# Attention block of a fused attention and convolution kernel: q.k products summed by adding DMAs, residual rows added by DMA, eight tiles in flight

## What is computed

```python
xn = groupnorm(x); xc = einsum('bchw,oc->bohw', xn, ciw) + cib
t  = xc as tokens (8 batch, 4096 pixels, 64 channels) + pe
tn = layernorm(t); q, k, v = tn @ wq.T + bq, ...; q2, k2, v2 = q @ wiq.T + biq, ...   # 8 heads of 8
scores = einsum('inhd,jnhd->nhij', q2, k2) / sqrt(8)      # for each pixel n: 8 images i against 8 images j
z  = softmax(scores) @ v2 ; z = z @ wout.T + bout ; t = z + t
a  = layernorm(t) @ w1.T + b1 ; g = t @ w2.T + b2
t  = a * gelu(g) @ w3.T + b3 + t
x  = einsum('bchw,oc->bohw', t, cow) + cob + x            # the residual
for _ in range(3):
    x = x + (conv(relu(conv(x, w1) + b1), w2) + b2) / 3
return relu(x)
```

## Time and profile before

| | us |
|---|---|
| median of 3 runs | 1139.01 |
| lowest, highest | 1138.61, 1140.38 |
| span of the profiled execution | 1136.3 |
| set-up block | 0 to 44.3 |
| attention block | 44.3 to 604.7 |
| convolutions | 604.7 to 1136.3 |

### The profile page before, as it was taken

How to read it: one execution, slowest core, us unless ns; L and a number is a source line. 1 busy time by engine, 2 the same in 40 slices (tenths; PEclk the granted TensorE clock), 3 DMA queues, 4 the chain that set the end, 5 groups by cost and what they waited for, 6 DMA issues and landing times. The chain is left out here.

```text
span 1136.3 us, 21019 instructions
## 1 busy us (share of the span) xinstructions
PE 1071.2 (94%) x7238; PEld 601.7 (53%) x7238; DVE 1039.7 (92%) x1475; ACT 652.5 (57%) x1525; POOL 510.7 (45%) x422
## 2 busy tenths in 40 slices
PE   4269999999999999999999999999999999999996
PEld 3156787778777777777653333333333333333331
DVE  5459999999999999999988999999999999999996
ACT  4568889888888888888743233253244242342333
POOL 5134564456445544554452424435345344444440
PEclk9999999999999999999999999999999999999998
DMA  8110111111111111110000000030001100030003
GB/s 303 54 37 21 39 29 35 32 39 29 33 35 38 29 31 38 38 29 20 20 20 1 1 1 1 1 75 1 1 1 34 41 1 1 1 74 1 1 1 74
DMA packets 87545, 35.83 MB, mean 32 GB/s; under 512 B 70210, under 2 KB 86851, under 8 KB 86931
## 3 DMA queue, kind: packets, MB, share of 16 engines
q1 hardware_dynamic: 85634, 33.81, 11.1%
q0 software_dynamic: 768, 0.33, 0.2%
q10 hardware_dynamic: 1040, 0.35, 0.1%
HBM read 26.09 MB, written 8.39 MB: 30 GB/s over the span
## 5 line engine op out<-in xcount | busy, mean ns | idle before, releaser
L1173 ACT ACTIVATE y<-banks,cols 128x1024 f32<-128x1024 f32 x96 | 110.3, 1208 | 259.8 <-PE banks L1165 259.8
L900 POOL TENSOR_TENSOR rstd<-var,half 128x8 f32<-128x8 f32 x32 | 80.8, 2526 | 216.5 <-DVE var L755 216.5
L1155 PE MATMUL banks<-mixed_h,cwp 128*128 128x512 f32 x384 | 177.6, 605 | 0.0
L1155 PE MATMUL banks<-early,cwp 128*128 128x512 f32 x372 | 169.2, 602 | 0.5 <-PEq L420 0.5
L1456 POOL TENSOR_TENSOR early<-xs 128x256 f32<-128x256 f32 x95 | 77.1, 811 | 160.1 <-DVE xs L1204 160.1
L1181 DVE TENSOR_TENSOR y<-y,banks 128x512 f32<-128x512 f32 x192 | 119.9, 682 | 15.2 <-ACT y L1173 15.0
L558 PE MATMUL banks<-consts,early 128*128 128x128 f32 x1024 | 133.2, 279 | 0.0
L1189 DVE TENSOR_TENSOR y<-y,banks 128x512 f32<-128x512 f32 x192 | 124.4, 685 | 8.7 <-PE banks L1165 6.5
L577 PE MATMUL banks<-consts,prod 128*128 128x128 f32 x1024 | 128.2, 273 | 2.8 <-DVE prod L526 2.1
L1155 PEld LDWEIGHTS banks<-mixed_h,cwp 128*128 128x128 f32 x384 | 69.0, 189 | 107.9 <-issue 107.9
L558 PEld LDWEIGHTS banks<-consts,early 128*128 128x128 f32 x1024 | 114.3, 144 | 18.8 <-issue 18.1
(11 more groups left out here) (184 smaller groups left out, 1868.8 us busy)
## 6 DMA issues: line engine op xcount, KB each, us to landing
xs<-in_x SPq DMA_DIRECT2D x4, 2048.0 KB, 16.5
xa<-in_x SPq DMA_DIRECT2D x32, 256.0 KB, 2.8
xr<-in_x SPq DMA_DIRECT2D x64, 128.0 KB, 2.8
out_y<-xs SPq DMA_DIRECT2D x32, 256.0 KB, 4.5
cw<-in_L_conv_w POOLq DMA_DIRECT2D x2, 144.0 KB, 3.9
consts<-in_consts ACTq DMA_DIRECT2D x1, 192.0 KB
group<-in_consts SPq DMA_DIRECT2D x1, 64.0 KB
w1n<-in_L_conv_w ACTq DMA_DIRECT2D x1, 64.0 KB
```

The costliest lines, as they stand in the source:

```text
L900: pool.tensor_tensor(rstd1[:, :], var1[:, :], top["half"][:, :], ALU.pow).then_inc(rstd1_done, 1)
L1155: pe.matmul(psum[PSUM_PAIR[v, q, j]][i][:, :, :], weights(v, i, j).rearrange("p n o -> p (n o)"), mixed[v][i][:, s0:s0 + WIDE, j, :], star ...
L1173: act.activation(pairs(y[i][q][:, :, :]), m1, ACT.Identity, bias=cols[:, (6, 8)[v]:(7, 9)[v]]).then_inc(m1_out[i][q], 1)
```

## The change

- **q.k sum.** `dve_p1` still makes 8 planes per piece. POOL then issues, for each piece, a DMA that adds planes 4 to 7 onto planes 0 to 3 inside SBUF (`pool_e_add`: 128 partitions of 2 KB). `pe_scores_t` waits for it and sums 4 planes in place of 8: 16 matmuls per tile in place of 32.
- **Residual.** `dve_x`, `sp_xr` and the `xr` buffers go. ACT copies the result with its bias into `xs` (`act_x`, two instructions of 128x256), then two DMAs per tile issued by POOL add x's rows from memory onto `xs` (`pool_residual`: 64 partitions x 8 images, runs of 256 B). POOL's block ends with a wait for the last of them.
- **Eight tiles in flight** in place of five; `run` calls 39 iterations. `dve_p1` moves whole into one iteration, the transposes come two iterations later.
- **Buffers.** `tt` and `qkv` 5, `z1` 3; `prod1` 6 pieces and `prod2` 5 pieces in rotation, with a semaphore per piece.
- **Order.** All five lists are new; `pe_av` takes its pieces in the order 2, 1, 0, 3. The work for the first convolution hangs at other places of the last iterations.

The diff, cut to its core:

```diff
+        STAGES = 8
+        T_RING, QKV_RING, Z1_RING = 5, 5, 3
+        P1_SLOTS, P2_SLOTS = 6, 5
...
         def pe_scores_t(pe, t, b):
...
-            wait(pe, p1_dve, DUOS * t + b + 1)
-            for e in range(HD):
-                m = pe.matmul(b2[:, P * b:P * (b + 1)], prod1[:, e, P * b:P * (b + 1)], ident,
-                              start=(e == 0), stop=(e == HD - 1), is_transpose=True)
+            wait(pe, e_added[b][t % 2], 16 * (t // 2 + 1))
+            for e in range(HD // 2):
+                m = pe.matmul(b2[:, P * b:P * (b + 1)], p1_slot(t, b)[:, e, :], ident,
+                              start=(e == 0), stop=(e == HD // 2 - 1), is_transpose=True)
...
+        def pool_e_add(pool, t, b):
+            wait(pool, p1_dve[b], t + 1)
+            v = p1_slot(t, b)
+            pool.dma_start(v[:, 0:HD // 2, :], v[:, HD // 2:HD, :], accum_op=ALU.add).then_inc(e_added[b][t % 2], 16)
+
+        def act_x(act, t, d):
+            wait(act, cow_mm, t + 1)
+            act.activation(x_view(t, d), x_psum(d), ACT.Identity, bias=cols[:, 4:5]).then_inc(x_done[d], 1)
+
+        def pool_residual(pool, t):
+            for d in range(2):
+                wait(pool, x_done[d], t + 1)
+            for r in range(2):
+                wait(pool, residual[r], 16 * t)
+                pool.dma_start(xs[half(r), :, t, 1:1 + HW], x_rows[:, :, 2 * t + r, :], accum_op=ALU.add)\
+                    .then_inc(residual[r], 16)
...
+            last, old = user(t, b, P1_SLOTS)
+            wait(dve, scoresT_mm[old], last + 1)
...
-        def dve_x(dve, t, k, d):
...
-            wait(dve, cow_mm, t + 1)
-            dve.scalar_tensor_tensor(x_view(t, d), x_psum(d), cols[:, 4:5], xr_view(k, d), ALU.add, ALU.add).then_inc(x_done[d], 1)
```

More of the change, by code:

```diff
@@ L711, in act_scale @@
                 wait(act, raw_out[g], t + 1)
+            v = qkv[t % QKV_RING]
             for i in range(B):
-                act.activation(qkv[k][:, i, :], qkv[k][:, i, :], ACT.Identity, scale=rstd1[:, i:i + 1]).then_inc(scaled_out, 1)
+                act.activation(v[:, i, :], v[:, i, :], ACT.Identity, scale=rstd1[:, i:i + 1]).then_inc(scaled_out, 1)
         def act_scores_t(act, t):
-            wait(act, scoresT_mm, DUOS * (t + 1))
+            for b in range(DUOS):
+                wait(act, scoresT_mm[b], t + 1)
             wait(act, scores_mm, t)
@@ L724, in act_z @@
         def act_z(act, t):
-            wait(act, av_mm, DUOS * (t + 1))
+            for b in range(DUOS):
+                wait(act, av_mm[b], t + 1)
             wait(act, z1_mm, t)
@@ L796, in dve_attn @@
             wait(dve, rden_done, t + 1)
-            wait(dve, p2_dve, DUOS * t)
+            for b in range(DUOS):
+                wait(dve, p2_dve[b], t)
             r = rden[:, :].unsqueeze(2).broadcast_to([P, C, B])
@@ L872, in free_for @@
             if i == 0:
-                wait(eng, scoresT_mm, DUOS * TILES)
-            else:
-                wait(eng, p2_dve, DUOS * (TILES - 1))
+                for b in range(DUOS):
+                    wait(eng, scoresT_mm[b], TILES)
+            else:
+                for b in range(DUOS):
+                    wait(eng, p2_dve[b], max(t + 1 for t in range(TILES) if t % QKV_RING >= OWN_QKV))
             wait(eng, edges_zeroed, 1)
         def written(eng, c):
-            for d in range(2):
-                wait(eng, x_done[d], 8 * (c + 1))
+            for r in range(2):
+                wait(eng, residual[r], 16 * 8 * (c + 1))
         def outer_ahead(dve, pieces):
@@ new lines, in pe_iteration, with act_iteration @@
+            if tiles[5]:
+                pe_rstd2(pe, t - 5)
+        def act_iteration(act, t, tiles):
+            if tiles[4]:
+                act_exp(act, t - 4)
+            if tiles[0]:
+                act_t(act, t)
+            if tiles[5]:
+                act_centered(act, t - 5)
+                act_square2(act, t - 5)
+            if tiles[7]:
+                act_x(act, t - 7, 0)
+                act_x(act, t - 7, 1)
+            if tiles[6]:
+                act_gelu(act, t - 6, 0)
+            if tiles[0]:
+                act_squares(act, t, 0)
+            if tiles[6]:
+                act_gelu(act, t - 6, 1)
+            if tiles[0]:
+                act_raw(act, t, 0)
+            if tiles[3]:
+                act_scores_t(act, t - 3)
+            if tiles[1]:
+                act_scale(act, t - 1)
+            if tiles[0]:
+                act_squares(act, t, 1)
+            if tiles[5]:
+                act_rrep(act, t - 5)
+            if tiles[0]:
+                act_raw(act, t, 1)
+            if tiles[4]:
+                act_z(act, t - 4)
@@ L1075, in _ @@
             run(pool, pool_iteration)
+            for r in range(2):
+                pool.wait_ge(residual[r], 16 * TILES)
         @block.sync
```

378 lines of the change are left out of this document (176 added, 202 removed).

## The result

The changed kernel takes 1127.2 us (median, 1125.72 to 1128.13), the kernel before 1139.6 beside it: ratio 0.989, 95% interval 0.9876 to 0.9904. It is faster, as forecast, and inside the range; but it gained 12.4 us where 20 were forecast. The profiled execution has a span of 1125.4 us, 10.9 less than before.

What follows compares the result with a forecast made beforehand. The prediction took DVE to pace the attention block, PE close behind. Steady part -36.6, ramp +12 and tail +5 gave -19.6 us on the 1136.3 span, 1116.7, plus 2.7 for the median: 1119 us, range 1101 to 1170.

Steps and rivals of the forecast that it cites:

- The bound: Attention block, steady part: DVE sets the pace, idle 0.43 us per tile, with PE close behind; PE's relief alone brings at most 0.43.
- TensorE's load: Transposes of pe_scores_t in the attention: 16 fewer per tile, about -2.0 us, leaving PE busy some 14.3 us.
- VectorE: DVE in the attention: dropping dve_x takes 0.78 us per tile off, 15.85 to 15.07; floor 14.8 to 15.07.
- ScalarE: ACT in the attention: two added activations cost 0.65 us per tile, 14.21 to 14.86; period cannot fall below about 14.9.
- POOL: POOL in the attention: six DMA issues per tile cost 4.0 us, 0.57 per add and 0.84 per x, 8.54 to 12.5.
- rival A: POOL's queue becomes the bound, slower than before: 1162 us at twice the issue price, about 1300 at full proportion; chance 0.18.
- rival B: Adding DMAs in the attention need over 15.1 us per tile, not the expected 4.5 to 11.5; 1178 at 17 us; chance 0.05.
- The period: Time per tile in the steady attention: 16.28 to 15.1 us (14.9 to 15.5), -36.6 us over 31 steps.
- C: New attention order meshes badly, DVE or ACT stopping each tile: period 15.4 to 16.3, 1141 us at 15.8; chance 0.15.
- D: Ramp cheap and self-waits gone: period 14.8 (-46 us), ramp +5, tail +3, 1101 us or less; chance 0.05.
- The ramp: Stretch before z1 of tile 0: late first p1 +4.9 us and a deeper pipeline +7, together +12 (+5 to +25).
- The tail: From z1 of tile 31 to the first convolution matmul: residual DMA's 0.84 issue and 3.9 landing, +5 us (3 to 6).

Runs made afterwards that it cites:

- Experiment 7: The kernel before with x written by ScalarE (act_x) instead of VectorE and x's input rows not added: 1138.9 us, period 16.28.
- experiment 6: The kernel before with only four of eight q.k planes transposed and summed, nothing added to them: 1129.1 us, period 15.876.
- experiment 4: The changed kernel without the adding DMAs of q.k, so PE sums 8 planes again with 32 matmuls per tile: 1162.7 us, period 16.527.
- experiment 1: The changed kernel with dve_var1 moved behind dve_z1 in DVE's list, nothing else: 1123.0 us, period 14.924.
- experiments 1 and 9: The 9 is the changed kernel with dve_var1 behind dve_z1 and the last two tiles' residual added by DVE: 1113.4 us, period 14.938.
- Experiment 3: The changed kernel with the last two tiles' x rows added by VectorE from rows loaded ahead, other tiles unchanged: 1118.9 us.

## Why the forecast was right in sign and 8 us short

**The bound.** Wrong. "DVE is the pace-maker (0.43 us idle per tile) and PE is close behind" has the two the wrong way round. I had both rows: PE's loads stop 0.76 us per tile for z1, DVE stops 0.27 for z1's products. I took the engine with the longer stop for the one that follows; but z1 goes from PE to DVE and back to PE, and two engines that hand work to each other both show a stop. Experiment 7 (VectorE relieved, 0.00) and experiment 6 (TensorE relieved, -0.40) decide it. The 0.43 that I gave as the most for PE's relief held for another reason than the one I named: it is the distance to the second limit. The period's way down, as far as the runs split it:

| step | period | by |
|---|---|---|
| before | 16.28 | TensorE and its hand-offs |
| 16 transposes fewer | 15.88 | VectorE, 148.5 of 150 |
| x by ScalarE | 15.70 | hand-offs in the old order |
| new order, eight tiles, buffers, the real DMAs | 15.13 | VectorE, 150 of 150, 0.5 of it held |
| `dve_var1` not held | 14.92 | TensorE, VectorE, ScalarE at 98% |

**TensorE's load.** -2.0 forecast. In the new order experiment 4 against after has PE busy 16.30 and 14.76 us per tile, -1.5. (The ends are modelled; in the kernel before PE counted as busy throughout. By the transposes' own times it is -2.0: 1.06 and 1.09 us for two pieces each, where 4.13 stood.)

**VectorE.** The move of x took 0.71 us off DVE (145.83 to 139.27 of 150, times 16.28), 0.78 forecast. The floor was put at 14.8 to 15.07; with the instruction free DVE is busy 14.69 (experiment 1), 0.1 below it. That it stands at 15.13 in the kernel after is the held `dve_var1`, in no step of mine: I had named the stretched bias as POOL's loss and never asked which of DVE's instructions can be the later one.

**ScalarE.** 14.86 forecast, 14.81 measured; `act_x` in the old kernel +0.57 (130.88 to 136.15), +0.65 forecast. "The period cannot fall below about 14.9": experiments 1 and 9 ended at 14.92 and 14.94.

**POOL and rival A.** POOL 12.5 forecast, 12.22 busy, but by two errors that cancel, which is luck. The issues were put at 4.0 us and take 5.95: 0.86 to 0.91 for an add where 0.57 stood, 1.15 to 1.19 for one of x where 0.84 stood. That is half as much again, though far from in proportion to the runs. The other three instructions were left at 8.54 and take 6.06: rstd1 1.66, rstd2 2.00, bias 2.40. In the kernel before, bias met one of DVE's products and took 3.44; in the new order DVE's max, gated values and difference run beside it, which read PSUM, and it takes about what it takes alone (2.34). The issues did not stretch either: two of x take 2.38 beside DVE's products and 2.30 with DVE idle. POOL waits for DVE's products (3 us in the period shown), not the reverse. Rival A falls, with less room than its 4.0 us of issues suggested.

**The DMAs and rival B.** 0.69 of 15.13 is 10.4 us of DMA time per tile, within 4.5 to 11.5 and near its upper end, that of three passes. The adds land after 4.1 to 4.2 us, against 8 to spare; there is no wait for them among the largest of the middle. Rival B falls.

**The period and rivals C and D.** 15.1 forecast, 15.13 measured; -36.6 forecast, -35.1 measured. The number came out right although its reason, relief of the pace-maker, was wrong: the busy times of PE, DVE and ACT in experiment 1 lie within 0.1 us of each other, so whichever was taken as the bound gave nearly the same end. That is luck. So is how close it came: without the held instruction, which the forecast did not have, the period is 14.92, and the unforeseen 0.2 us brought it to the 15.1. The order did not mesh badly (C): with its tiles and buffers, and the short transposes, it took 0.57 us off. D fell with the ramp. (The rivals' chances add to 0.04 for the same and 0.29 for slower, not 0.05 and 0.28.)

**The ramp.** +12 forecast, +13.1 measured. The first p1 starts at 66.21 (about 66 forecast); from there to z1 of tile 0 are 38.4 us, 30.4 before: +7.9 for +7. The granted clock falls there too (to 0.66 in a window of 5 us), which I had not foreseen; what it costs was not measured.

**The tail.** This is the mis-sized term: +5 (3 to 6) forecast, +9.4 measured, with +1.7 in the convolutions behind it that I had at zero. "0.84 issue and 3.9 landing" left out that the issue waits for the landing of the tile before (1.87), that there are two issues (2.30 together) and that the landing is a wait of 4.97 from there: 9.1 in place of 4.74. And it missed what an engine idle for 8.3 us brings on, the slow start. Experiment 3 gives back 8.3 of the 11.1 that tail and convolutions lost. Add the four errors, 1.5 for the period, 1.1 for the ramp, 4.4 for the tail and 1.7 for the convolutions, and the 8.7 us by which the span of 1125.4 stands over 1116.7 are found.

## What to carry to other kernels

Two engines that hand a tile back and forth both show a stop for the other, so the rows don't say which one paces: relieve each alone, and read the one whose relief moves the period. What a relief is worth depends on what else has been relieved: the move of x brought 0.00, 0.18, 0.26 or 0.46 us per tile. When a final transfer replaces a final instruction, count the chain behind the last result (the wait for the transfer before, every issue, the landing) and ask what the idle time does to TensorE's clock; the last tiles may well go the old way, at no cost to the steady part. Look in every list for small instructions that stand beside a long one of GpSimd: one of eight columns cost half a microsecond per tile, and another place or another form gives it back.

## What the runs showed of the hardware

- A `tensor_scalar` of 128x8 from SBUF to SBUF took 0.16 us alone and 0.68 or 1.54 beside a bias of POOL, in each case until its end; a `tensor_reduce` in the same place took 0.15.
- The same bias took 2.34 us beside a mostly idle DVE and 3.44 in the kernel before, where it starts together with a product of DVE of 1.21 us. In the kernel after it is listed with 3.81, but from the end of the issue ahead of it 2.40, beside instructions of DVE that read PSUM.
- Issuing an adding DMA of 128 x 2 KB within SBUF took POOL 0.86 to 0.91 us, one of 512 runs of 256 B from memory 1.15 to 1.19, both from end to end; they landed after 4.1 and 5.6 us. The lengths in the profile overlap: by the page's means of 1.24 and 1.97 us the six issues of a tile would be 8.9 us, by their ends they are 5.95, by their starts 4.1.
- The granted clock fell to 0.50, 1.2 GHz, after PE had been idle for 8.3 us. In the ramp it fell to 0.69, 0.66 and 0.74; in the windows ahead of the first two PE had been busy 3.40 and 2.53 of 5 us, with stops between. The windows from 85 to 90, 100 to 105 and 105 to 110 us of the kernel after:

```profile
85.00:90.00 5.00, 2.78 (x24) 2.33 (x24) 4.22 (x5) 3.73 (x16) 4.25 (x2) 0.69 0.42 81
...
100.00:105.00 5.00, 4.52 (x40) 3.41 (x40) 2.73 (x5) 1.11 (x2) 1.66 (x1) 0.66 0.00 0
105.00:110.00 5.00, 3.02 (x18) 2.27 (x20) 4.83 (x7) 2.11 (x6) 0.90 (x1) 0.74 0.48 105
```
